# A vision tower on one core: in the third stage the transposes of the expert sums stand in the next step, and the gates behind the third scores

## The reference

```python
# end of layer 0: each token's two expert outputs, weighted and summed
moe = jnp.einsum('ebsd,bse->bsd', ye, w)
x = _ln(moe + x, ln3_g, ln3_b)
h = h + x
# layer 1, on _layernorm(h): attention over 32 keys to either side, 8 heads of 16
qkv = (x @ w_qkv + b_qkv).reshape(B, S, 3, H, hd)
scores = jnp.einsum('bshd,bswhd->bshw', q, k_win) * scale
attn = jax.nn.softmax(jnp.where(valid, scores, -1e9), axis=-1)
out = jnp.einsum('bshw,bswhd->bshd', attn, v_win).reshape(B, S, D)
h = h + (out @ w_out + b_out)
# layer 1, on _layernorm(h): one of 16 linear maps for each image, times its gate
scores = jax.nn.softmax(jnp.mean(x, axis=1) @ Wg + bg, axis=-1)
idx = jnp.argmax(scores, axis=-1)
h = h + gate[:, :, None] * (jnp.einsum('bsd,bdo->bso', x, We[idx]) + be[idx][:, None, :])
```

## Time and profile before

| | us |
|---|---|
| median of three runs | 3073.66 |
| lowest and highest | 3069.62, 3074.09 |
| the profiled execution | 3065.54 |
| its span, first to last instruction | 3063.6 |

### The profile page before, as it was taken

How to read it: one execution, slowest core, us unless ns; L and a number is a source line. 1 busy time by engine, 2 the same in 40 slices (tenths; PEclk the granted TensorE clock), 3 DMA queues, 4 the chain that set the end, 5 groups by cost and what they waited for, 6 DMA issues and landing times.

```text
span 3063.6 us, 85773 instructions
## 1 busy us (share of the span) xinstructions
PE 2778.5 (91%) x31087; PEld 2160.1 (71%) x31087; DVE 1981.9 (65%) x4482; ACT 1844.8 (60%) x3693; POOL 1314.0 (43%) x1252
## 2 busy tenths in 40 slices
PE   6999999999999994899999968999999999999997
PEld 4666666666666663799999956777777777777775
DVE  4888888888888886222222215777777777777775
ACT  4776777777677774344444435666666666666664
POOL 1355555555655555000000026555555555555540
PEclk9999999999999997999999988999999999999998
DMA  3122222222222211677777741111111111111110
GB/s 130 70 78 95 85 83 83 77 77 77 89 90 83 83 32 52 211 231 226 228 230 229 229 141 39 54 50 46 46 47 46 46 45 47 46 45 45 46 34 28
DMA packets 139576, 284.73 MB, mean 93 GB/s; under 512 B 25440, under 2 KB 82784, under 8 KB 135392
## 3 DMA queue, kind: packets, MB, share of 16 engines
q1 hardware_dynamic: 114912, 245.77, 24.9%
q0 software_dynamic: 24576, 37.80, 4.5%
HBM read 215.18 MB, written 68.29 MB: 93 GB/s over the span
## 4 chain that ended last, share of the span: by engine, by line
issue 26%; PE 21%; POOL 10%; DMA 2%; ACT 1%; DVE 0%; POOLq 0%; SPq 0%; DVEq 0%; ACTq 0%
POOL ycho L1429 5%; PE psum L1519 4%; PE psum L1477 3%; PE psum L1494 3%; POOL ysum L1442 3%; PE psum L1502 2%; PE psum L1542 2%; PE psum L1529 2%; DMA ycho<-expert_out,place 2%; PE psum L1554 1%; POOL qdiag L1450 1%; PE psum L1515 1%; PE psum L1572 1%; PE psum L1482 1%; POOL ycho L1437 1%
## 5 line engine op out<-in xcount | busy, mean ns | idle before, releaser
L1429 POOL DMA_INDIRECT ycho<-expert_out,place x384 | 358.9, 935 | 664.7 <-issue 651.3
L1013 POOL DMA_INDIRECT expert_in<-rows,slot_i x384 | 445.3, 1160 | 130.5 <-issue 108.0
L1182 ACT ACTIVATE hid<-psum,w_blk 128x256 f32<-128x256 f32 x608 | 268.9, 473 | 326.9 <-PE psum L1139 326.9
L1725 ACT ACTIVATE ex<-psum,smin 128x96 f32<-128x96 f32 x1152 | 295.3, 341 | 158.2 <-DVE smin L1805 155.2
L483 PE MATMUL psum<-xn,w_in 128*128 128x288 f32 x1024 | 299.3, 416 | 31.7 <-ACT rf L697 27.7
L1450 POOL TENSOR_TENSOR qdiag<-qs,parity 128x128 f32<-128x128 f32 x288 | 117.7, 414 | 422.8 <-PE psum L1519 267.1
L1148 PE MATMUL psum<-w_blk,hid 128*128 128x128 f32 x2432 | 296.7, 275 | 0.0
L1812 DVE RECIPROCAL inv<-psum 128x64 f32<-128x64 f32 x288 | 159.0, 552 | 209.4 <-PE psum L1554 209.3
L1139 PE MATMUL psum<-x_t,w_blk 128*128 128x256 f32 x1216 | 289.5, 381 | 2.2 <-DMA w_blk<-w_exp_in 2.2
L989 POOL TENSOR_TENSOR unit<-unit 128x576 f32<-128x576 f32 x64 | 129.3, 2021 | 370.3 <-ACT unit L650 262.6
L1148 PEld LDWEIGHTS psum<-w_blk,hid 128*128 128x128 f32 x2432 | 283.9, 192 | 0.1
(11 more groups left out here) (237 smaller groups left out, 6031.7 us busy)
## 6 DMA issues: line engine op xcount, KB each, us to landing
w_blk<-w_exp_in SPq DMA_DIRECT2D x152, 578.0 KB, 4.0
xin<-x_in SPq DMA_DIRECT2D x32, 1716.0 KB, 7.2
rows_in<-expert_in SPq DMA_DIRECT2D x152, 128.0 KB, 2.4
expert_out<-rows_out SPq DMA_DIRECT2D x152, 128.0 KB, 3.3
h_dram<-h SPq DMA_DIRECT2D x32, 288.0 KB
x_dram<-x SPq DMA_DIRECT2D x32, 288.0 KB, 2.1
h1c<-h_dram SPq DMA_DIRECT2D x32, 288.0 KB, 3.0
x2c<-x_dram SPq DMA_DIRECT2D x32, 288.0 KB, 3.3
```

Source lines behind the costliest of these rows:

```text
L1013: pool.indirect_dma_start(out=expert_in[:, :], out_offset=bass.IndirectOffsetOnAxis(ap=slot_i[z.s][:, n:n + 1], axis=0), in_=rows[z.s][:, ...
L1182: nc.scalar.activation(hid[b.s][:, c, :], HB[b.s][c % HK], ACT.Gelu_apprx_tanh, bias=w_blk[b.q][:, FF + FC * D + c:FF + FC * D + c + 1]).t ...
L1429: pool.indirect_dma_start(out=ycho[x.s][:, k, :], out_offset=None, in_=expert_out[:, :], in_offset=bass.IndirectOffsetOnAxis(ap=place[x.s] ...
L1725: done = nc.scalar.activation(ex[u % RING][:, b, :], score_bank(u)[:, b * KW:(b + 1) * KW], ACT.Exp, bias=smin[u % RING][:, b:b + 1], scal ...
```

## The change

PE's transposes of the expert sums move from the end of the step of an item to the middle of the step behind it: they are no longer `moe(v, A0)` but `moe(w, A0)`. DVE's addition `prec` moves with them, from the head of the step to behind the last heads of `y`. The gates of `z` write the same bank, and so move behind the third scores and wait for `prec`. Each instruction is still there once for each item.

```diff
@@ c_tensor, step
                     pe.wait_ge(xq_ready, x.upto(1, 1))
                     query_or_key(x, 0, A1)
-                    if w:
-                        pe.wait_ge(prec_ready, w.upto(1, 1))
                     values_in(x, 0, A0)
...
                 if y:
                     values(y, 8)
+                if w:
+                    if x:
+                        pe.wait_ge(k_ready, x.upto(1, 1))
+                    moe(w, A0)
                 if x:
                     scores(x, 1)
+                    scores(x, 2)
+                if w:
+                    pe.wait_ge(prec_ready, w.upto(1, 1))
                 if z:
                     gates(z, A0)
-                if x:
-                    scores(x, 2)
...
                 if x:
                     scores(x, 8)
                     turn(x, 6)
-                if v:
-                    if w:
-                        pe.wait_ge(norm4_act, w.upto(3, 2))
-                    elif v.old(1):
-                        pe.wait_ge(prec_ready, v.upto(1, 0))
-                    moe(v, A0)
                 if x:
                     values(x, 5)
@@ c_vector, step
                 if v_:
                     row_numbers(v_)
-                if w:
-                    v.wait_ge(moe_done, w.upto(1, 1))
-                    v.wait_ge(h_landed[w.s], 32 * w.n + 32)
-                    v.tensor_tensor(two(prec[:]), both(A0), two(x2c[w.s][:]), ALU.add).then_inc(prec_ready, 1)
...
                 if y:
                     halves(y, 8)
                     heads(y, 8)
+                if w:
+                    v.wait_ge(moe_done, w.upto(1, 1))
+                    v.wait_ge(h_landed[w.s], 32 * w.n + 32)
+                    v.tensor_tensor(two(prec[:]), both(A0), two(x2c[w.s][:]), ALU.add).then_inc(prec_ready, 1)
                 if x:
                     minimum(x, 1)
```

## The result

The changed kernel takes 3093.68 us (median of 6 runs, 3092.61 to 3094.12), the kernel before 3072.32 (6 runs, 3067.89 to 3074.09): the ratio is 1.0072, 95% interval 1.0062 to 1.0083. The forecast was 3071.2, range 3061 to 3088: wrong, and on the side of the slower rival, which gave 3086. Of the runs further down, two executions (4373 us of the kernel before with all late, 4524 us of the kernel before with POOL's multiply behind the choice) ran at a granted clock of 0.60 and 0.58 as a mean; the ratios leave them out, and without them the medians given would be 1.0 and 0.2 us lower.

The account below looks back on a forecast made before the run. PE, busy 91%, bounds the kernel, idling mostly for `ysum` (65.1 us). Full steps keep 37.55; ramp -3.6, finding the beat +1.0, first step without `v` +0.2 give -2.4: median 3073.66 becomes 3071.2, range 3061 to 3088.

Parts of the forecast that it names:

- the slower rival: Low clock follows PE's restart or never lies in the wait: full steps 38.05 against 37.5, total 3086; chance 0.15.
- The end of the step: From `turn(x, 6)` to the next query: PE waits for `xq` instead, idle 0.6 and 2.05; gains 0.4 us.
- The transposes in the middle: Six transposes between `values(y, 8)` and `scores(x, 1)`, where PE had no wait: adds 0.5 us a step.
- If the low stretch begins with the query ... 38.05: At the query: all 3.41 us of low clock behind it cost 1.7, making the step 38.05 against 37.5.
- With 1.0 us of it in the wait the cost is 1.2 ... it stands still there: At the query: steps slide against falls 37.55 apart until 1.0 us of low clock lies in PE's wait; step 37.55.
- The ramp, -3.6: First queries of the third stage no longer stand behind waiting transposes: 3.6 us gained as the full steps begin.
- "Cost nothing" for the gates and `prec`: Mid-step: `prec` behind `heads(y, 8)` and gates behind the third scores are free, less than 0.2 us if `prec` is late.
- The faster rivals: Two cases at the step's end: `xq` ready early, 2975 us, chance 0.05; clock staying up, 3039 us, chance 0.09.
- `xq` not late: At the step's end DVE gets its multiply through ahead of `ysum`: step 34.3, total 2975 us; chance 0.05.
- Clock up: Two shorter waits at the step's end keep the clock up: step 36.35, total 3039 us; chance 0.09.

Follow-up runs that it names:

- all late: DVE makes the last `one_head`, `minimum` and `xq` before residual, `heads` multiply and rest of the map's choice: changed kernel 0.9923, kernel before 1.0035.
- POOL's multiply behind the choice: POOL's multiply by the weights also waits for the third instruction of DVE's choice of the map: changed kernel 1.0104, kernel before 1.0043.
- gates back: Changed kernel with its gates back behind the second scores, transposes and `prec` left in their new places: ratio 1.0127 to the kernel before.
- the choice late: Last six instructions of the choice of the map moved behind `xq` on DVE: changed kernel 0.9937, kernel before 1.0072.

## Why the prediction was wrong, step by step

- **The end of the step.** Right. Waits of 0.52 and 2.04 where 0.6 and 2.05 were forecast, `xq` ready 1.2 us after `ysum`, the query 3.22 after PE's stop there and 3.15 to 3.43 in the full steps (forecast 3.28).
- **The transposes in the middle.** Right. From the query at 2417.98 PE works until 2452.07 + 0.64 = 2452.71, which is 34.73, less 1.7 for the low stretch 33.0: 0.44 over 32.58 (forecast 0.5).
- **"If the low stretch begins with the query ... 38.05".** Right: 38.08, 38.07 and 38.12 in the three steps from 2417.98.
- **"With 1.0 us of it in the wait the cost is 1.2 ... it stands still there".** This is the step that failed. The steps did slide back against falls 37.55 apart (2418.96, 2456.51, 2494.05, 2531.60), and up to a lead of 0.57 the part of the low stretch in the wait did cost nothing (the step behind the fall at 2340.45, which led by 0.57, is the shortest of the full ones, 37.79). But the lead of 1.0 at which the step was to stand still was never reached. At leads of 0.65 to 0.84 the low stretch became twice as long, 6.83, cost 3.0 us in place of the 1.3 that 3.41 less a lead of 0.8 would have cost, and the next fall came 40.96 later. The pattern began anew, and no step came down to 37.55. The prediction took the length of a low stretch as fixed at 3.41, because every one in the full steps of the kernel before had it; there the falls led the query by as much (0.87 in the earlier trace rows), but PE was at the transposes and values under them, and after the change it is idle. The slower rival had the right step, 38.05; the longer stretches added 0.28 to it, 7 us in 26 steps, which took the result past it and out of the range.
- **The ramp, -3.6.** Mis-sized to nothing. The first query did come 3.4 us sooner, counted from POOL's first gather (39.17 against 42.57). But the low stretch that it stands in lasted 47.79 in place of 44.37, and at the third query 0.4 of the gain was left (107.29 against 107.68), at the fourth none (144.00 against 143.85).
- **"Cost nothing" for the gates and `prec`.** Right in the first measurements, in which no gate wait shows in the full steps. In the experiments' conditions it was 9 to 14 us by the medians, and 0.25 us in a step without low clock.
- **The faster rivals.** `xq` not late: out, until DVE is reordered. Clock up: out; with the two gaps, 0.52 and 2.04, every full step has its fall.

What the runs show: the change moves PE's wait for `ysum` to `xq`, gains 0.4 us at the step's end, pays 0.44 for the transposes, and has more of each low stretch behind the query (up to all 3.41 us in place of 2.54, so up to 0.43 more of cost). On top of that come the six doubled stretches. The doubled stretch was not made or taken away by an experiment, and that it comes from the lead over an idle PE is read off the traces alone. Two of the later kernels had it once each in front of a query of their full steps, where the fall led the query by 0.65 (the changed kernel unedited) and 0.64 us (with gates back). In the full steps of all three kernels, and of the changed one with POOL's multiply behind the choice, falls that led by 0.58 or less brought 3.41 us. The window of the long stretch in the unedited changed kernel of the later measurements:

```profile
2815.21:2822.04 6.83, 6.17 (x49) 5.10 (x50) 2.22 (x7) 4.04 (x12) 2.47 (x5) 0.50 0.49 156
```

These eight stand ahead of a query with PE idle before it. But a lead over 0.6 is no rule for other places. In the kernel before with the choice late, one fall led PE's next matmul by only 0.39 (2314.41, after 2.39 us of idle time) and the low clock lasted as long:

```profile
2314.02:2320.85 6.83, 6.44 (x111) 4.88 (x114) 2.92 (x11) 2.66 (x10) 1.34 (x2) 0.50 0.30 94
```

And while the stage fills, 16 of the 18 kernels of the experiments have one stretch of 6.83, with leads of 0.28 to 1.00. All have in common that PE was idle at the fall; what makes the chip hold the low clock longer there stays open.

## What to carry to other kernels

Before a wait is moved away from one engine's sum, list every instruction between that sum and the next use on the same chain: here the transposes and `xq` both hung on it, and only one was moved. Ask also what the moved work costs where it stands: inside a wait it was free, in mid-step it cost 0.4. A small instruction of a few elements that takes microseconds was here the sign that another engine held it; try such instructions behind the one that the bound engine waits for, and see what they now delay. Then try the change again, and hold it against the best kernel without it: its ratio turned from 1.007 to 0.988 once DVE had the new order in both kernels, while the lowest ratio of all kernels that leave nothing out was still one without the change. And a clock stretch that is seen at one length only is no constant that a sum may be built on.

## What was not expected of the hardware

- Low stretches of 6.83 us in full steps where the others were 3.41: eight times in three traces with the fall 0.64 to 0.84 us ahead of PE's restart, once with it 0.39 ahead.
- Instructions of 4 x 16 elements on DVE took 1.4 to 2.8 us beside POOL's arithmetic, 0.21 and 0.22 without it. POOL pays too: the same addition takes 1.8 us where DVE is held by it once and 2.85 where DVE's residual and multiply come beside it.
- The same program took 3072 us in the first measurements and 3144 to 3186 on chips 0, 4, 7 and 12. The later traces have pauses of PE of 0.2 and 0.4 us at one fixed place of each step (L1529, laid to nothing that the profile shows, 15 to 19 us in sum), and the third stage of the kernel before is 81 us longer (1335.2 against 1253.7, from its first fall of the clock on). The cause was not found. The two kernels' ratio was 1.0072 in the first measurements and 1.0062 to 1.0073 in the later ones (against all 26 runs of the kernel before, and 3203.87 / 3180.76). So that the change makes the kernel slower does not hang on it, but the parts of the cost do.
